# Layer-norm statistics of a fused MoE tail: centred products with tokens on partitions, row sums on ScalarE, inverse roots on GpSimd, and the last products in two parts

## What is computed

```python
def _ln(x, g, b):
    mu = jnp.mean(x, axis=-1, keepdims=True)
    var = jnp.mean(jnp.square(x - mu), axis=-1, keepdims=True)
    return (x - mu) * jax.lax.rsqrt(var + EPS) * g + b

x1 = jnp.einsum('btd,hd->bth', x, sw1) + sb1
x2 = jnp.einsum('btd,hd->bth', x, sw2) + sb2
sh = _ln(jax.nn.silu(x1) * x2, s_ln_g, s_ln_b)            # hidden width 128
shared_out = jnp.einsum('bth,dh->btd', sh, sw3) + sb3
...
x_moe = x[index_b, index_t]
top1_idx = jnp.argmax(expert_scores + exp_bias, axis=-1)
...
z = _ln(jax.nn.silu(h1) * h2, sel_ln_g, sel_ln_b)
out_all = jnp.einsum('meh,edh->med', z, ew3) + eb3
...
final_out = shared_out.at[index_b, index_t].set(shared_moe_out + expert_moe_out)
```

## Time and profile before

| | us |
|---|---|
| median of 3 runs | 585.34 (584.84 to 585.60) |
| the profiled execution, its own time | 586.33 |
| its span in the trace | 584.40 |
| stage 2 in it (first product of stage 2 to the end) | 511.4 to 584.4 |
| busy share of PE, DVE, ACT, POOL over the span | 97%, 70%, 45%, 30% |

### The profile page before, as it was taken

One profiled execution on the slowest core, in us unless ns is written; L12 is line 12 of the kernel. 1 busy time (PEld: TensorE's weight loads), 2 busy tenths in 40 slices (PEclk: granted clock), 3 DMA queues, 4 the chain that ended last, 5 costly groups with the idle time before them and its releaser, 6 DMA issues.

```text
span 584.4 us, 16995 instructions
## 1 busy us (share of the span) xinstructions
PE 567.4 (97%) x5093; PEld 502.7 (86%) x5094; DVE 408.8 (70%) x1092; ACT 264.1 (45%) x577; POOL 177.2 (30%) x529
## 2 busy tenths in 40 slices
PE   5999999999999999999999999899999998999995
PEld 4888888885889999999999999799999997866784
DVE  4969986776846686777577688765747565568674
ACT  6665756732335343435343343343434343546450
POOL 0360000000563435352525333334342500387000
PEclk9999999999999999999999999899999999999996
DMA  8712245101000224220000000000000000291231
GB/s 266 258 73 73 72 148 175 56 2 36 2 2 22 91 94 125 79 105 38 2 2 3 2 2 3 2 3 2 3 1 3 3 4 4 89 361 60 73 121 66
DMA packets 28478, 36.90 MB, mean 63 GB/s; under 512 B 4762, under 2 KB 24115, under 8 KB 28132
## 3 DMA queue, kind: packets, MB, share of 16 engines
q1 hardware_dynamic: 28292, 35.57, 18.5%
q0 software_dynamic: 96, 0.20, 0.1%
HBM read 27.30 MB, written 8.53 MB: 61 GB/s over the span
## 4 chain that ended last, share of the span: by engine, by line
PE 96%; issue 1%; DVE 1%; ACT 1%; DMA 1%; POOL 0%; POOLq 0%
PE ps_hidden L1163 43%; PE ps_out L1191 42%; PE ps_hidden L594 4%; PE ps_hidden L643 1%; PE ps_out L614 1%; PE ps_hidden L678 1%; PE ps_out L1234 1%; PE ps_turn L627 1%; PE ps_out L606 1%; PE ps_small L627 1%; DMA W<-in_xT 1%; DVE X L784 1%; PE ps_turn L1241 0%; PE ps_small L1238 0%; PE ps_out L678 0%
## 5 line engine op out<-in xcount | busy, mean ns | idle before, releaser
L1191 PE MATMUL ps_out<-hbuf,W 128*128 128x242 f16 (+2 forms) x2304 | 250.6, 269 | 0.0
L1191 PEld LDWEIGHTS ps_out<-hbuf,W 128*128 (+1 forms) x2304 | 224.8, 98 | 18.3
L1732 POOL COPY xs<-X 128x88 f16 x352 | 127.2, 413 | 290.2 <-PE ps_hidden L1163 178.4
L1033 ACT ACTIVATE h<-ps_hidden,b 128x242 f32<-128x242 f32 (+1 forms) x384 | 155.7, 466 | 77.0 <-PE ps_hidden L1163 76.7
L1163 PE MATMUL ps_hidden<-xs,W 128*128 128x242 f16 x1536 | 165.9, 269 | 2.1 <-issue 2.1
L1163 PEld LDWEIGHTS ps_hidden<-xs,W 128*128 x1536 | 150.8, 98 | 12.3 <-issue 2.7
L1338 DVE TENSOR_TENSOR hbuf<-h,hbuf 128x484 f16<-128x484 f32 (+2 forms) x192 | 129.8, 676 | 7.5
L1619 DVE SCALAR_TENSOR_TENSOR acc<-ytmp,wrow,acc 128x44 f32 (+1 forms) x352 | 65.8, 259 | 94.4 <-ACT ytmp L1124 90.2
L1163 PE MATMUL ps_hidden<-X,W 128*128 128x256 f16 (+1 forms) x768 | 91.3, 280 | 8.8 <-DVE W L1322 6.0
L1336 DVE CAST hbuf<-h 128x484 f16<-128x484 f32 (+2 forms) x192 | 84.6, 440 | 17.9 <-ACT h L1033 16.9
L1163 PEld LDWEIGHTS ps_hidden<-X,W 128*128 128x128 f16 x768 | 75.9, 99 | 21.4 <-DVE W L1322 5.7
(11 more groups left out here) (291 smaller groups left out, 302.9 us busy)
## 6 DMA issues: line engine op xcount, KB each, us to landing
stage<-in_ew SPq DMA_DIRECT2D x16, 512.0 KB, 3.9
stage<-in_xR SPq DMA_DIRECT2D x8, 512.0 KB, 3.8
moved_rows<-stage SPq DMA_DIRECT2D x8, 512.0 KB, 2.6
X<-moved_rows SPq DMA_DIRECT2D x8, 512.0 KB, 9.2
out_rows<-X SPq DMA_DIRECT2D x16, 256.0 KB, 2.2
W<-in_xT SPq DMA_DIRECT2D x7, 512.0 KB, 9.2
W<-in_fw SPq DMA_DIRECT2D x1, 2304.0 KB, 12.3
W<-in_sw SPq DMA_DIRECT2D x4, 256.0 KB, 3.1
```

Of the source, the lines that this page charges most:

```text
L1033: i = nc.scalar.activation(h32[:, j, k * size:(k + 1) * size], ps1[j][:, k * size:(k + 1) * size], ACT.Gelu_apprx_tanh, bias=b1[:, bass.ds ...
L1191: mm = pe.matmul(out, w2(e, wp, hb, db), h, start=(n == 0), stop=(n == 3 * HB - 1))
L1732: i = nc.gpsimd.tensor_copy(xs[:, parity, :, j * SEG:(j + 1) * SEG], X[:, :, bass.ds(cols[j], SEG)])
```

## The change

Five things are changed, all of them in stage 2:

1. `centre(k)`: the roles of the operands are exchanged. The four 128-token blocks of g are now the weights, and `Cm` (128 columns) is what streams through, so that tokens stand on partitions. It makes eight products of 128 columns in place of two of 512. The results of odd steps go to the second `ps_out` bank.
2. `square(k)`: four instructions of 128 columns, each with a row sum as a second output (`accum_out` into `sums2`). `variance(k)` on PE is gone.
3. `roots(0)` and `roots(1)` are taken from DVE and given to POOL, behind `gather(0)`, as 15 linked instructions each. `rows(k)` for k < 4 waits for their semaphore `var_taken`.
4. `root(q)` on ACT reads the sums directly, with bias and scale in the instruction, and `root(0)` stands ahead of `square(7)`; DVE no longer copies the sums out (`late_roots_in` is gone).
5. The one-hot is transposed after `gfirst(0, 4)` in step 7 and into another bank; `take_hot` stands ahead of `rows(3)`. `pick` comes ahead of `second(6)`, then `gvariance`, four of the nine products of `gsecond`, `second(7)` and the other five; `mixed` is cut in the same way around `rows(7)`.

```diff
             def square(k):
                 act.wait_ge(c_done, k + 1)
-                if k >= 2:
-                    act.wait_ge(var_mm, k - 1)
-                nc.scalar.activation(sq[:, k % 2, :], psy[0], ACT.Square).then_inc(sq_ready, 1)
+                for n in range(MG):
+                    i = nc.scalar.activation(sq[:, k % 2, n * P:(n + 1) * P], psy[k % 2][:, n * P:(n + 1) * P],
+                                             ACT.Square, accum_out=sums2[:, k * MG + n:k * MG + n + 1])
+                i.then_inc(sq_ready, 1)
...
             def root(q):
-                act.wait_ge(var_taken, q + 3)
-                nc.scalar.activation(tms, tms, ACT.Sqrt).then_inc(root_made, 1)
+                act.wait_ge(sq_ready, 2 * q + 6)
+                two = slice((2 * q + 4) * MG, (2 * q + 6) * MG)
+                nc.scalar.activation(roots2[:, two], sums2[:, two], ACT.Sqrt, bias=epss,
+                                     scale=WS * WS / FH).then_inc(root_made, 1)
...
+            root(0)
             square(NQ - 1)
-            root(0)
...
             def centre(k):
                 pe.wait_ge(g_ready, k + 1)
-                if k >= 1:
-                    pe.wait_ge(sq_ready, k)
-                else:
+                if k >= 2:
+                    pe.wait_ge(sq_ready, k - 1)
+                elif k == 0:
                     pe.wait_ge(late_done, 2)
-                for part in range(2):
-                    mm = pe.matmul(psy[0], Cm, ghl[:, k % GR, part, :], start=(part == 0), stop=(part == 1))
+                for n in range(MG):
+                    for part in range(2):
+                        mm = pe.matmul(psy[k % 2][:, n * P:(n + 1) * P], ghl[:, k % GR, part, n * P:(n + 1) * P], Cm,
+                                       start=(part == 0), stop=(part == 1))
                 mm.then_inc(c_done, 1)
...
             centre(NQ - 1)
-            variance(NQ - 2)
             second(4)
-            variance(NQ - 1)
             second(5)
             for n in range(3):
                 gcentre(0, n)
-            second(6)
-            second(7)
-            turn_hot(0)
-            gvariance(0)
             pe.wait_ge(w3s_in, 16)
             pe.wait_ge(ce8_in, 16)
             pick(0)
-            gsecond(0)
+            second(6)
+            gvariance(0)
+            gsecond(0, 0, 4)
+            second(7)
+            gsecond(0, 4, NJ)
...
             def rows(k):
                 dve.wait_ge(x_rows_in[k], 16)
                 dve.wait_ge(u_done, k + 1)
+                if k < 4:
+                    dve.wait_ge(var_taken, k // 2 + 1)
...
-                if k == 3:
-                    roots(0)
                 if k == 4:
                     rows(0)
                 if k == 5:
-                    roots(1)
                     rows(1)
...
-            late_roots_in(2)
+            take_hot(0)
             rows(3)
...
+            def roots(q):
+                taken = [q * 14]
+
+                def link(i):
+                    taken[0] += 1
+                    i.then_inc(root_step, 1)
+                    pool.wait_ge(root_step, taken[0])
+
+                pool.wait_ge(sq_ready, 2 * q + 2)
+                two = slice(2 * q * MG, (2 * q + 2) * MG)
+                out = rstd[:, two]
+                link(nc.gpsimd.tensor_scalar(tms, sums2[:, two], 1.0 / FH, EPS, ALU.mult, ALU.add))
+                link(nc.gpsimd.tensor_scalar(out.bitcast(I32), tms.bitcast(I32), -0.5, MAGIC, ALU.mult, ALU.add))
+                for n in range(3):
+                    link(nc.gpsimd.tensor_tensor(qms, out, out, ALU.mult))
+                    link(nc.gpsimd.tensor_tensor(qms, qms, tms, ALU.mult))
+                    link(nc.gpsimd.tensor_scalar(qms, qms, -0.5, 1.5, ALU.mult, ALU.add))
+                    link(nc.gpsimd.tensor_tensor(out, qms, out, ALU.mult))
+                nc.gpsimd.tensor_scalar(out, out, 1.0 / WS, None, ALU.mult).then_inc(var_taken, 1)
...
                 gather(0)
+                roots(0)
+                roots(1)
                 pool.wait_ge(out_done, 16 * NH)
                 scatter(0)
```

More of the change, by code:

```diff
@@ L359, in program @@
         qms = stf[:, 876:876 + 2 * MG]
+        sums2 = stf[:, 884:884 + NQ * MG]
+        roots2 = stf[:, 916:916 + NQ * MG]
+        epss = stf[:, 948:949]
         ohT = stf[0:FE, 1024:1024 + P]
@@ L667, in pick, with gsecond @@
             def pick(g):
-                pe.wait_ge(hot_taken, g + 1)
+                pe.wait_ge(sq_ready, NQ)
                 pe.matmul(psy[1][:, D:2 * D], ohT, ce8, start=True, stop=True).then_inc(pick_mm, 1)
-            def gsecond(g):
-                for j in range(NJ):
+            def gsecond(g, lo=0, hi=NJ):
+                if lo == 0:
+                    pe.wait_ge(gsq_ready, g * 3 + 2)
+                for j in range(lo, hi):
                     if j == 4:
@@ L686, in stage2_pe @@
                 centre(k - 1)
-                if k >= 2:
-                    variance(k - 2)
                 if k >= 4:
@@ L700, in stage2_pe @@
                     gfirst(0, 4)
+                    turn_hot(0)
             centre(NQ - 1)
-            variance(NQ - 2)
             second(4)
-            variance(NQ - 1)
             second(5)
@@ L724, in group @@
                     gcentre(g, n)
+                pick(g)
                 gvariance(g)
-                pick(g)
                 gsecond(g)
@@ L731, in stage2_dve @@
         def stage2_dve(dve, link, late_store):
-            def inverse_root(step, out, tm, qm):
-                step(nc.vector.tensor_scalar(out.bitcast(I32), tm.bitcast(I32), -0.5, MAGIC, ALU.mult, ALU.add))
-                for n in range(3):
-                    step(nc.vector.tensor_tensor(qm, out, out, ALU.mult))
-                    step(nc.vector.scalar_tensor_tensor(qm, qm, -0.5, tm, ALU.mult, ALU.mult))
-                    step(nc.vector.scalar_tensor_tensor(out, qm, 1.5, out, ALU.add, ALU.mult))
             def c_low(k):
@@ L776, in late_roots @@
                 dve.wait_ge(root_made, q - 1)
-                link(nc.vector.reciprocal(rstd[:, two], tms))
+                link(nc.vector.reciprocal(rstd[:, two], roots2[:, two]))
             def rows(k):
@@ L854, in groots, with picked, mixed @@
                 glink(nc.vector.tensor_tensor(rstdg[:, 0:1], rstdg[:, 0:1], rm[:, 3:4], ALU.mult))
-            def mixed(g):
-                dve.wait_ge(gu_done, g * 5 + 1)
-                nc.vector.scalar_tensor_tensor(moe, last_bank(0), rstdg[:, 0:1], moe, ALU.mult,
-                                               ALU.add).then_inc(moe_step[0], 1)
+            def picked(g):
                 dve.wait_ge(pick_mm, g + 1)
                 nc.vector.tensor_scalar(moe2, psy[1][:, D:2 * D], rm[:, 4:5], None, ALU.mult).then_inc(moe_step[1], 1)
-                for j in range(1, NJ):
+            def mixed(g, lo=0, hi=NJ):
+                if lo == 0:
+                    dve.wait_ge(gu_done, g * 5 + 1)
+                    nc.vector.scalar_tensor_tensor(moe, last_bank(0), rstdg[:, 0:1], moe, ALU.mult,
+                                                   ALU.add).then_inc(moe_step[0], 1)
+                for j in range(max(lo, 1), hi):
                     if j % 2 == 0:
@@ L905, in stage2_dve @@
             rows(4)
-            late_roots_in(3)
             rows(5)
+            picked(0)
             late_roots(3)
             rows(6)
+            groots_in(0)
+            groots(0)
+            mixed(0, 0, 4)
             rows(7)
-            groots_in(0)
-            take_hot(0)
-            groots(0)
-            mixed(0)
+            mixed(0, 4, NJ)
             end()
@@ L923, in group @@
                 take_hot(g)
+                picked(g)
                 groots_in(g)
```

40 lines of the change are left out of this document (12 added, 28 removed).

## The result

| | before | after |
|---|---|---|
| runs side by side, first comparison | 585.09 (584.83 to 585.60) | 589.11 (588.32 to 589.66) |
| ratio, first comparison | | 1.0064 [1.0037, 1.0092] |
| the same kernels again, 17 and 12 runs | 586.38 (582.62 to 587.67) | 589.25 (585.79 to 590.89) |
| ratio, second comparison | | 1.0052 [1.0027, 1.0077] |
| the profiled execution, its span | 586.33, 584.40 | 588.32, 586.5 |

The changed kernel is slower by about 0.6%, 3 to 4 us. The forecast was 587.9, slower, with a range of 584.9 to 591.0.

A forecast was written before the change was run, and what follows sets the result against it. PE, busy 97%, bounds the kernel. Gains of 6.3 - 0.5 on PE and about 3 in the tail, less 7.4 pause and 1 at `take_hot`, give span 584.3; half clock adds 2.7: median 587.9, range 584.9 to 591.0.

The forecast's parts named there:

- Part 1, centre: PE's queue in stage 2: the new `centre` takes 0.50 a step, between 0.45 and 0.83.
- Part 2, the squares: ACT: four squares with sums take 1.2, between 0.8 and 1.6; ACT falls behind PE by tenths of a microsecond.
- Part 3, the roots behind the gather: `roots(0)` on POOL, queued behind the gather, takes 4.65; PE pauses 7.4 us and begins `second(1)` 4.67 later.
- a quicker gather nothing: POOL's gather in stage 2: no gain was counted for DVE's small instructions going away beside POOL's copies.
- A rule against the change: The skill's 1.96 times applied to POOL's root steps: `roots(0)` takes 5.9 in place of 4.65, median 589.1.
- Part 4, to the tail: From the pause to the end: `centre(7)` at 562.4, `second(4)` at 564.5, 1 given back at `take_hot`, span 584.3.
- Part 5, the clock: PE at half clock for 5.5 us from `second(1)` on, 2.7 lost; span 587.0, median 587.9.
- The tail's clock: Rival, chance 0.18: the clock also falls in the tail at `gvariance`, about 6 us at half, 2.9, so 590.8.
- From the span to the median: Whole kernel: a span of S stands for a median of S + 0.94.
- the 3 expected in the tail: End of stage 2: a gain of about 3 us, where the half clock is gone.
- a sign that the clock may hold through such a wait: Rival, chance 0.17: the clock holds through PE's pause, as over a wait of 2.8 us; 585.2, no change.

The follow-up runs named there:

- the run with the roots inside the gather: The changed kernel with `roots(0)` on POOL after the 96th of the gather's 128 copies; 591.06, ratio 1.0077 to the kernel before.
- the run that kept PE busy: The changed kernel with 28 unused products of 512 columns on PE ahead of `second(1)`; 587.97, ratio 1.0029 to the kernel before.

## Why the prediction was right, point by point

The sign, its cause and the order of size were right: 587.9 against 589.1 and 589.25, inside the range. The steps, against the two profiles of the changed kernel:

- **Part 1, centre.** Foretold 0.50 a step, between 0.45 and 0.83. The eight products stand from 536.48 on, each 0.056 behind the last: 0.45. The line through the earlier trace rows down to 128 columns, 0.056 each, was exact here; the 0.05 I put on top was not needed.
- **Part 2, the squares.** Foretold 1.2, between 0.8 and 1.6. ACT's timeline of after, the first and the last of the four and what follows:

```profile
529.68 0.28 ACT L503 ACTIVATE W<-ps_out 128x128 f32<-128x128 f32 x1
529.85 0.19 ACT L503 ACTIVATION_READ_ACCUMULATOR W<-ps_out 128x1 f32 x1
...
530.60 0.22 ACT L503 ACTIVATION_READ_ACCUMULATOR W<-ps_out 128x1 f32 x1
530.70 0.65 ACT L511 ACTIVATE W<-W 128x512 f16<-128x512 f32 x1
```

  The row sum is an instruction of its own, but overlaps the next square; four squares with sums take 530.70 - 529.68 = 1.02. PE does not wait for ACT in steps 1 to 4, and ACT, whose step of 3.11 (two `silu` at 528.11 and 531.22) equals PE's, did not fall behind as the sum had it. Only DVE's `g_low` waits 0.26 a step for ACT, which costs nothing.
- **Part 3, the roots behind the gather: the mechanism was right, two of its sizes were high.** POOL's steps follow each other at 0.28, not 0.31 (15 take 4.2, not 4.65), and the gather ended 25.30 behind the first product of stage 2 (before: 25.99), 0.69 earlier, where I had given "a quicker gather nothing". With the roots on DVE it ended at 25.79, so about 0.5 of the 0.69 come with their leaving DVE. PE idled from 536.93 to 543.64, 6.7 instead of 7.4; `second(1)` came 3.86 later than before instead of 4.67. Its waits, its releaser and who stood behind it are as foretold: ACT's `g_high(5)` waited 6.00, and that cost nothing, since `first(6)` started without a wait.
- **A rule against the change.** A step on 128x8 has 0.20 on POOL against the 0.17 of the earlier trace rows on DVE, 1.2 times as much; the twelve of `roots(0)` on DVE in the profile of before take 0.16 to 0.21, so that some are no shorter than POOL's. The Trainium skill (GPSIMD Engine Reference, 3. Performance versus the Vector engine) has 1.96 times at 2048 elements; no run here is at that size, and for eight elements a partition the measurement decides: its estimate of 5.9 was too high beside an idle DVE. Beside a busy one (5.6 in the run with the roots inside the gather) another place bears on it. The Trainium skill (GPSIMD Engine Reference, 1. Specifications) says that GpSimd shares its SBUF interface with VectorE and contends with DVE instructions of two SBUF inputs. `c_low` is one, and the steps of 1.25 to 1.92 agree; the prediction did not weigh that.
- **Part 4, to the tail.** Foretold `centre(7)` at 562.4 without the clock, `second(4)` at 564.5, 2.1 behind it. It was 1.75 behind. The size of the delay, about 1, was right (0.28 at `centre(7)` and 1.14 at `second(4)`), its cause was not: `take_hot` costs 0.2, as the run without it ahead of `rows(3)` shows, and what `centre(7)` and `rows(3)` wait for is `g_low(7)`, behind a chain on ACT. ACT's and DVE's timelines of after:

```profile
558.60 1.28 ACT L523 ACT_TABLE_LOAD   x1
559.89 0.21 ACT L523 ACTIVATE stage<-stage 128x9 f32<-128x9 f32 x1
560.12 1.28 ACT L497 ACT_TABLE_LOAD   x1
561.41 0.69 ACT L497 ACTIVATE W<-ps_hidden,fb 128x512 f32<-128x512 f32 x1
```
```profile
563.68 0.69 DVE L749 SCALAR_TENSOR_TENSOR W<-W 128x512 f16<-128x512 f32 x1 [0.80 <-ACT W L511]
564.30 0.27 DVE L813 COPY stage<-ps_hidden 8x128 f32<-8x128 f32 x1
564.50 0.85 DVE L764 SCALAR_TENSOR_TENSOR X<-ps_turn,stage,X 128x256 f32<-128x256 f32 x2
```

  Two table loads of 1.28 stand around the router's activation (L523), and `silu(7)` (L497) comes behind them, 3.66 behind the start of `first(7)`. In the profile of before that chain is the same (3.67), and `g_low(7)` starts 5.84 behind `first(7)` there and 5.93 here: the chain is no longer than it was, and the longer `square(6)` adds 0.1 at most. What changed is PE, which has two variances (1.6) less to do between `first(7)` and `second(4)` and so reaches the chain earlier. PE's old, longer queue had covered it; I never priced it.
- **Part 5, the clock.** I took 2.7 for 5.5 us at half behind the pause. The first profile has 3.6 us, and the run that kept PE busy gives 1.7; the second has 5.1 us, 2.5. So the term was right for one run and high by 1.0 for another: it has no single size. The Trainium skill (TensorE: Matmul & The Clock Gate, Part 1) says that the same kernel shows a different number of products at half clock from run to run; the two profiles agree.
- **The tail's clock.** My forecast had it at full speed and priced a fall, as a rival with 0.18, at 2.9. It fell in one of the two profiles of the changed kernel and in five of the seven others with the same `gvariance`; the price is 23.69 - 22.06 = 1.6. The chance was too low and the price too high. With the overestimated pause this nearly cancels, which is luck: stage 2 was foretold with 75.7 and measured with 74.3 and 76.65.
- **From the span to the median.** That 587.9 is only 1.2 below the median is a sum of misses with both signs, and in part luck. In the first profile stage 2 is 1.4 shorter than foretold, it begins 0.94 later than in the profile of before, and the median stands 2.61 above the span where I had taken 0.94: the profile of before is of an execution slower than all three of its runs (586.33), that of after of the fastest of four (588.32). In the second profile stage 2 is 0.9 longer than foretold and begins 0.99 later, and the median stands only 0.35 above the span. What bears on the later beginning of stage 2 is in the last section.

The same accounts say why a change that takes 6.3 us of work off the bounding engine (eight variances of 0.81, less eight times 0.02 for `centre`) loses 3 to 4: the pause gives 6.7 back, the clock behind it 1.7 to 2.5, the waits on `g_low(7)` and `rows(3)` 1.4; and the 3 expected in the tail are the clock's and come only in some runs. Against the one profile of before, whose tail had lost 3.3 to the clock, stage 2 is 1.2 and 3.5 longer in the two profiles; the accounts give about 0.9 less in both, which stays unassigned.

## What to carry to other kernels

Before an instruction block is moved to an idle engine, look up when that engine is done with what stands ahead of it in its queue, and who is the first to wait for the block: here 0.2 us instructions on an idle engine cost 6.7 us because they were queued behind a gather. The pauses of 6.55 us in TensorE (three profiles) and of 3.67 us (one, with one of 2.58 shortly ahead of it) were each followed by half clock for another 3.6 to 5.1 us, which cost 1.7 to 2.5 us more behind the long ones; so cheap work is better left on the engine that reaches it early. And one profile is one draw where the clock is concerned: count stretches at half clock in several profiles before a difference of 1 to 3 us is given a cause.

## What the runs showed of the hardware that I had not expected

- **Short pauses of PE are followed by a half clock in some runs and not in others.** Stage 1, which is the same in every kernel here, has two: one of about 2.1 us at about 374, behind 20 products of four columns, and one of 2.5 to 3.1 at about 487. Behind the first, the same 48 products in the profile of before and in the second one of after:

```profile
375.96 6.82 PE L1163 MATMUL ps_hidden<-xs,W 128*128 128x242 f16 x48 [2.15 <-issue]
```
```profile
376.39 5.16 PE L1168 MATMUL ps_hidden<-xs,W 128*128 128x242 f16 x48 [2.14 <-issue]
```

  It fell there in 10 of 13 profiles, and behind the second pause in 8 of 13. In the five profiles with both, stage 2 began at 512.20 to 513.85 (median 513.32), in the eight with one at 511.26 to 513.04 (median 512.30)., which I had taken as a sign that the clock may hold through such a wait, was one draw of these. What decides it within one kernel stays open.
- **The time of a run goes with these draws.** The runs of the kernel before at a mean clock of 0.999 took 582.6 to 583.4, those at 0.986 to 0.991 took 586.1 to 589.9. The clock is not all of it: at 0.996 there are runs of 583.5 and of 587.0. That spread is wider than the whole effect of the change, and only many runs side by side separate the kernels.
- **A POOL instruction of 0.20 takes 1.25 to 1.92 when a `c_low` runs beside it on DVE**, and 0.52 to 0.58 beside a `g_low`. Both read two inputs from SBUF, and POOL's instruction ends 0.05 to 0.06 behind DVE's in all nine cases (above).
